# Two layer norms in a block-pipelined transformer tower: mean dropped, variance by ScalarE square with accumulator instead of VectorE statistics

## What is computed

```python
def _layernorm(x, axis=-1, eps=1e-5):
    m = jnp.mean(x, axis=axis, keepdims=True)
    v = jnp.var(x, axis=axis, keepdims=True)
    return (x - m) / jnp.sqrt(v + eps)

h = _L0_tok_ref(x, sqrt_eig, pct, 64)       # spectrum x Legendre table, then an inverse real FFT: [64, 256, 512]
h = h + _L0_attn_ref(_layernorm(h), K, temperature, bias)   # tanh logits, band of 12, softmax
h = h + _L0_ffn_ref(_layernorm(h), W, b)    # adds two one-hots in columns 128 to 159 of the marked rows
```

## Time and profile before

| | |
|---|---|
| three runs | 1578.57, 1577.88, 1573.31 us |
| the profiled execution | 1565.4 us; its span, first to last instruction, 1563.6 us |
| busy, share of the span | PE 89%, DVE 69%, ACT 43%, POOL 39% |
| stage 2's loop | about 497 to 1249 us of the span |
| mean granted clock of TensorE | 0.954 of full speed |

### The profile page before, as it was taken

How to read it: one execution, slowest core, us unless ns; L and a number is a source line. 1 busy time by engine, 2 the same in 40 slices (tenths; PEclk the granted TensorE clock), 3 DMA queues, 4 the chain that set the end, 5 groups by cost and what they waited for, 6 DMA issues and landing times. The chain is left out here.

```text
span 1563.6 us, 31624 instructions
## 1 busy us (share of the span) xinstructions
PE 1388.2 (89%) x9389; PEld 1217.4 (78%) x9389; DVE 1084.1 (69%) x2564; ACT 676.4 (43%) x1373; POOL 614.5 (39%) x1598
## 2 busy tenths in 40 slices
PE   4777777767999999999999999999999996599993
PEld 3666666657999999999999999999999995355541
DVE  1322222217899999999999999999999984466662
ACT  1222222213455455455455455455454452366672
POOL 2000000001466556655555665565565565121221
PEclk9799989988999999999999999999999998699997
DMA  9999999972122122212211211211221111000000
GB/s 374 428 428 428 428 428 429 428 265 71 56 78 73 70 69 74 77 68 69 80 68 68 81 68 68 81 68 68 74 75 68 43 42 42 23 9 8 8 3 3
DMA packets 58746, 210.57 MB, mean 135 GB/s; under 512 B 9412, under 2 KB 12176, under 8 KB 46288
## 3 DMA queue, kind: packets, MB, share of 16 engines
q1 hardware_dynamic: 47360, 172.29, 28.2%
q10 hardware_dynamic: 5200, 33.62, 5.4%
q0 software_dynamic: 6144, 4.14, 0.9%
HBM read 138.73 MB, written 73.07 MB: 135 GB/s over the span
## 5 line engine op out<-in xcount | busy, mean ns | idle before, releaser
L187 PE MATMUL s1b<-pg,cg 128*128 128x256 f32 x1024 | 246.9, 403 | 90.0 <-DVE cg L138 85.7
L187 PEld LDWEIGHTS s1b<-pg,cg 128*128 128x128 f32 x1024 | 204.9, 203 | 131.5 <-ACT stage L215 46.6
L426 PE MATMUL ps_kx<-xThi,Khi 128*128 128x256 f32 x1024 | 283.7, 277 | 4.0 <-DVE xTlo L678 4.0
L427 PE MATMUL ps_kx<-xTlo,Khi 128*128 128x256 f32 x1024 | 283.4, 277 | 0.0
L428 PE MATMUL ps_kx<-xThi,Klo 128*128 128x256 f32 x1024 | 283.4, 277 | 0.0
L138 DVE TENSOR_TENSOR cg<-xg,se 128x2048 f32<-128x2048 f32 x32 | 73.3, 2292 | 233.3 <-DMA pg<-in_pct_dram 211.0
L585 ACT ACTIVATE o<-h,sh,sc 128x512 f32<-128x512 f32 x128 | 97.5, 809 | 266.7 <-POOL sh L818 266.7
L426 PEld LDWEIGHTS ps_kx<-xThi,Khi 128*128 128x128 f32 x1024 | 193.2, 189 | 4.6 <-DVE xTlo L678 4.6
L428 PEld LDWEIGHTS ps_kx<-xThi,Klo 128*128 128x128 f32 x1024 | 192.9, 188 | 0.0
L427 PEld LDWEIGHTS ps_kx<-xTlo,Khi 128*128 128x128 f32 x1024 | 192.9, 188 | 0.0
L215 ACT COPY stage<-s1b 128x512 f32<-128x512 f32 x128 | 65.7, 598 | 234.0 <-PE s1b L187 234.0
(11 more groups left out here) (138 smaller groups left out, 3216.9 us busy)
## 6 DMA issues: line engine op xcount, KB each, us to landing
pg<-in_pct_dram SPq DMA_DIRECT2D x32, 2048.0 KB, 27.7
xg<-in_xs_dram SPq DMA_DIRECT2D x32, 1024.0 KB, 22.9
spec<-stage ACTq DMA_DIRECT2D x64, 512.0 KB, 8.5
xt<-spec SPq DMA_DIRECT2D x64, 512.0 KB, 3.6
out_dram<-o SPq DMA_DIRECT2D x64, 512.0 KB, 2.8
recs<-rec POOLq DMA_DIRECT2D x16, 160.0 KB, 16.1
recs<-rec,idx POOLq DMA_INDIRECT x128, 2.3
Kf<-in_K_dram SPq DMA_DIRECT2D x1, 1024.0 KB, 23.6
```

The source lines that it names most:

```text
L187: last = nc.tensor.matmul(bank[(b % 2) * 4 + m // 2][:, m % 2, :], cg[:, b % 2, m * 2 + h, :], pg[:, b, m * 2 + h, :], start=(h == 0), sto ...
L426: nc.tensor.matmul(out_ap, whi, mhi, start=(j == 0), stop=False)
L427: nc.tensor.matmul(out_ap, whi, mlo, start=False, stop=False)
```

## The change

Both norms take the mean as zero. The variance is the mean of the squares, made by two ScalarE activations for each sample and norm (Square of the row scaled by 1/sqrt(512), its sum accumulated into one column). For h2 these stand in ACT's slot after pThi and before xnhi; for h they stand at the end of ACT's slot, after o and before the next slot's tanh. All bn_stats and bn_aggr leave DVE, `off` leaves POOL, and xn and x2 are one multiplication without the subtraction.

```diff
+        squares = sb("squares", [P, 2, TILES, NLON])
+        var1 = sb("var1", [P, 4, TILES])
+        var2 = sb("var2", [P, 2, TILES])
+        zeros = sb("zeros", [P, TILES])
...
@@ ScalarE, slot: after pThi, before xnhi
+                if has(i - 2):
+                    n = i - 2
+                    act.wait_ge(dve_h2, n * 2 + 2)
+                    wait(act, pool_sc2, (n - 1) * 2)
+                    wait(act, act_var2, n * 2)
+                    for t in range(TILES):
+                        nc.scalar.activation(squares[:, 1, t], h2[:, k % 2, t], ACT.Square, scale=1.0 / math.sqrt(NLON),
+                                             accum_out=var2[:, k % 2, t:t + 1]).then_inc(act_var2, 1)
...
-                    act.wait_ge(pool_sc2, n * 3 + 3)
+                    act.wait_ge(pool_sc2, n * 2 + 2)
...
@@ ScalarE, slot: after o, last
+                if has(i + 2):
+                    n = i + 2
+                    act.wait_ge(dve_h, n * 3 + 3)
+                    wait(act, pool_rstd1, n - 3)
+                    wait(act, act_var1, n * 2)
+                    for t in range(TILES):
+                        nc.scalar.activation(squares[:, 0, t], h[:, (k + 2) % 4, t], ACT.Square, scale=1.0 / math.sqrt(NLON),
+                                             accum_out=var1[:, (k + 2) % 4, t:t + 1]).then_inc(act_var1, 1)
...
@@ VectorE, slot
-                        nc.vector.tensor_scalar(xn[:, r2, t], h[:, r4, t], mv1[:, r4, t, 0:1],
-                                                rstd1[:, r4, t:t + 1], ALU.subtract,
+                        nc.vector.tensor_scalar(xn[:, r2, t], h[:, r4, t], rstd1[:, r4, t:t + 1], None,
                                                 ALU.mult).then_inc(dve_xn, 1)
...
-                        nc.vector.bn_stats(bn2[:, t, :], h2[:, r2, t]).then_inc(dve_bn2, 1)
...
-                        nc.vector.bn_aggr(mv2[:, r2, t, :], bn2[:, t, :]).then_inc(dve_mv2, 1)
...
-                        nc.vector.bn_stats(bn1[:, t, :], h[:, r4, t]).then_inc(dve_bn1, 1)
...
-                        nc.vector.bn_aggr(mv1[:, r4, t, :], bn1[:, t, :]).then_inc(dve_mv1, 1)
...
-                        nc.vector.tensor_scalar(x2[:, r2, t, :], h2[:, r2, t, 0:P], mv2[:, r2, t, 0:1],
-                                                rstd2[:, r2, t:t + 1], ALU.subtract,
+                        nc.vector.tensor_scalar(x2[:, r2, t, :], h2[:, r2, t, 0:P], rstd2[:, r2, t:t + 1], None,
                                                 ALU.mult).then_inc(dve_x2, 1)
...
+            nc.vector.memset(zeros[:, :], 0.0).then_inc(consts_set, 1)
...
@@ GpSimd, slot
-                    pool.wait_ge(dve_mv1, n * 2 + 2)
+                    pool.wait_ge(act_var1, n * 2 + 2)
...
-                    pool.wait_ge(dve_mv2, n * 2 + 2)
+                    pool.wait_ge(act_var2, n * 2 + 2)
...
-                    nc.gpsimd.tensor_tensor(off[:, :], mv2[:, r2, :, 0], rstd2[:, r2, :], ALU.mult).then_inc(pool_sc2, 1)
-                    pool.wait_ge(pool_sc2, n * 3 + 2)
-                    nc.gpsimd.tensor_tensor(sh2[:, r2, :], dcT[:, :, bass.ds(n, 1)].rearrange("p t o -> p (t o)"), off[:, :],
+                    nc.gpsimd.tensor_tensor(sh2[:, r2, :], dcT[:, :, bass.ds(n, 1)].rearrange("p t o -> p (t o)"), zeros[:, :],
                                             ALU.subtract).then_inc(pool_sc2, 1)
```

More of the change, by code:

```diff
@@ L1 @@
 from contextlib import ExitStack
+import math
 import numpy as np
@@ L296, in stage2_blocks @@
         sh2 = sb("sh2", [P, 2, TILES])
-        off = sb("off", [P, TILES])
         mx = sb("mx", [P, TILES])
@@ L328, in stage2_blocks @@
         pe_rank = sem("pe_rank")
+        act_var1 = sem("act_var1")
+        act_var2 = sem("act_var2")
         act_od = sem("act_od")
@@ L341, in stage2_blocks @@
         dve_h = sem("dve_h")
-        dve_bn1 = sem("dve_bn1")
-        dve_mv1 = sem("dve_mv1")
         dve_xn = sem("dve_xn")
@@ L351, in stage2_blocks @@
         dve_h2 = sem("dve_h2")
-        dve_bn2 = sem("dve_bn2")
-        dve_mv2 = sem("dve_mv2")
         dve_x2 = sem("dve_x2")
@@ L742, in slot @@
                     n, r4 = i + 1, (k + 1) % 4
-                    pool.wait_ge(dve_mv1, n * 2 + 2)
+                    pool.wait_ge(act_var1, n * 2 + 2)
                     settled(pool)
-                    nc.gpsimd.tensor_scalar(ve[:, 0, :], mv1[:, r4, :, 1], EPS, None, ALU.add).then_inc(pool_ve, 1)
+                    nc.gpsimd.tensor_scalar(ve[:, 0, :], var1[:, r4, :], EPS, None, ALU.add).then_inc(pool_ve, 1)
                     pool.wait_ge(pool_ve, (max(n - 3, 0) if isinstance(n, int) else n - 3) + n + 1)
@@ L805, in slot @@
                     n, r2 = i - 2, k % 2
-                    pool.wait_ge(dve_mv2, n * 2 + 2)
+                    pool.wait_ge(act_var2, n * 2 + 2)
                     settled(pool)
-                    nc.gpsimd.tensor_scalar(ve[:, 1, :], mv2[:, r2, :, 1], EPS, None, ALU.add).then_inc(pool_ve, 1)
+                    nc.gpsimd.tensor_scalar(ve[:, 1, :], var2[:, r2, :], EPS, None, ALU.add).then_inc(pool_ve, 1)
                     pool.wait_ge(pool_ve, n + 1 + (min(n + 4, NB) if isinstance(n, int) else n + 4))
@@ L815, in slot @@
                     nc.gpsimd.tensor_scalar(sc2[:, r2, :], rstd2[:, r2, :], 1.0, None, ALU.add).then_inc(pool_sc2, 1)
-                    nc.gpsimd.tensor_tensor(off[:, :], mv2[:, r2, :, 0], rstd2[:, r2, :], ALU.mult).then_inc(pool_sc2, 1)
-                    pool.wait_ge(pool_sc2, n * 3 + 2)
-                    nc.gpsimd.tensor_tensor(sh2[:, r2, :], dcT[:, :, bass.ds(n, 1)].rearrange("p t o -> p (t o)"), off[:, :],
+                    nc.gpsimd.tensor_tensor(sh2[:, r2, :], dcT[:, :, bass.ds(n, 1)].rearrange("p t o -> p (t o)"), zeros[:, :],
                                             ALU.subtract).then_inc(pool_sc2, 1)
-            pool.wait_ge(consts_set, 5)
+            pool.wait_ge(consts_set, 6)
             pool.wait_ge(dcT_set, 1)
```

## The result

The changed kernel took 1640.32 us (median of four runs, 1635.03 to 1643.13) against 1578.22 us (four runs of the kernel before, the three above and 1579.51): a ratio of 1.0399, 95% interval 1.0376 to 1.0422, so 62 us slower. Forecast were 1648 us, 70 us slower, in a range of 1620 to 1680. The profiled execution has a span of 1633.2 us.

What follows compares the result with a forecast made beforehand. Two bounds of about equal length were taken: PE's work, 14.67 us a slot, and the ACT-POOL ring, 14.64. Terms of 1.37 - 0.37 - 0.10 + 0.30 = 1.20 us a slot added 70 us to 1577.9: 1648 us, range 1620 to 1680.

Steps and rivals of the forecast that it cites:

- The ring: Stage 2's closed chain on ACT and POOL from one tanh to the next, 14.64 us; whatever lengthens it lengthens the slot.
- Squares of h: On ACT between o and the next tanh, in the ring: a pair adds 1.37 us, bounds 1.16 and 1.63.
- off: Subtraction leaving POOL between sc and sh, with the wait behind it, in the ring: -0.37 us a slot.
- lg: POOL's step after tanh, in the ring, no longer overlapped by DVE's xnlo: -0.10 us a slot.
- The build of h against POOL: POOL's second-norm ve (L808) meeting DVE's L665 and L667, in the ring: +0.30 us a slot.
- Full lock-out: Rival: L808 always held through both DVE instructions L665 and L667, 1.51 us a slot, 1667 us; chance 0.15.
- Squares of h2: On ACT after pThi: 1.37 us hidden in 3.96 us of idle time, xTlo 0.9 us ahead of PE's keys.
- DVE's 2.7 us less: bn_stats and bn_aggr leaving DVE, 2.7 us a slot, costed at nothing because the ring hardly waits for DVE.
- The sum: All terms in the ring together: 1.20 us a slot over 60 slots, less some 2 us.
- PE keeps the beat: Rival: a quicker POOL chain makes good the squares, PE's 14.67 us bounds again, 1573 us; chance 0.09.
- Table loads: Rival: ACT reloads its table around Square, 1.28 us a slot in the ring, 1725 us; chance 0.03.
- The clock: Rival: PE's waits lower its granted clock from 2.4 GHz, 18.3 us a slot at 0.80, 1790 us; chance 0.03.

Runs made afterwards that it cites:

- the light runs: Matmuls of Klo with the rounded rows left out of keys: kernel before without 16 a slot 1610.09 us, without 8 1580.34 us; changed kernel without 16 1662.86 us.

## Why the prediction was right, and where it was off

*The bound.* The ring was read rightly from the timelines: tanh follows the squares without idle time, moving the squares out of it takes the loss away, a second pair adds its length again, and PE's weight load for rank waits 1.19 us a slot where about 1.3 was forecast. What I wrote of PE was too high: "about 14.67 us when it waits for nothing". It is 14.57. I had subtracted only the wait for acc that the list named; in the trace the two halves of the first rank product start 0.13 us apart while PE waits there, and 0.03 in the kernel with the squares behind tanh: another 0.1 us, which I had taken for work. So the two bounds did not stand side by side: the ring alone held the kernel before, by 0.18 us a slot.

*Squares of h.* 1.37 us was forecast from the exps' pair and measured is 1.23 (0.61 a square): mis-sized by 0.14, inside its bounds of 1.16 and 1.63. A square of h takes 0.617 us, where exp's 0.502 and my 0.185 for the columns made 0.69.

*off* gave 0.37, as forecast; *lg* gave 0.08 of the 0.10: before, DVE's xnlo was still running for 0.29 us when it began (the slot of the earlier trace rows), and in the changed kernel xnlo is over by then. Before:

```profile
806.93 1.22 DVE L717 TENSOR_TENSOR xnlo<-xn,xnhi 128x1024 fp32r<-128x1024 f32 x1
```

*The build of h against POOL.* +0.30 was forecast as the middle between getting in between the two h instructions (0) and being held through both (+0.61), and +0.22 was measured. The way was a third one: ve does get in between, 0.08 us sooner than before, and rstd2, which I had not costed, is held by the second instruction for 0.30 us. That the size comes near is luck: it was a mean of two cases for ve, and what cost was rstd2. Full lock-out of the second ve (L808 before the change, L797 after), a rival with 0.15, is out: it ends 0.08 us behind the first of the two h instructions. The rule that I had quoted from the Trainium skill, "SBUF — State Buffer", section "Who interferes with whom", an exclusion for the length of one instruction, holds here: ve lies against the first and rstd2 against the second.

*Squares of h2* were hidden from PE's keys, as forecast: no wait of PE for xThi or xTlo appears. "0.9 us to spare" was a statement about those keys, though, and I had not followed the lateness to DVE's end of the slot; alone, this half costs 21 us. In the full change the late od is what brings the build of h onto rstd2, so the 0.30 us there is a price of these squares.

*DVE's 2.7 us less* were rightly costed at nothing: the kernel with the first norm alone changed does more on DVE and takes the same time. But they do keep the late od from making DVE late for lg, ve and nmx.

*The sum* was 1.20 us a slot and is 1.07. The four terms that were forecast measured 1.00 together; the 0.12 between keyhi and pos, which had no term, brings the total nearer, and that is luck too. *PE keeps the beat*: out, by 1.07 us. *Table loads*: out, the trace still has one load, and squares, tanh and o leave no gap that a second, of 1.283 us, would need. *The clock* stayed at 1.00, as forecast for this change; the light runs show that it was nearer than I had written, since it fell where PE's wait was 1.5 us a slot (72.3 us in 49 waits) instead of 0.99, and its price there, 32 us, comes in single slots and not as a mean. With the squares of h made twice it fell too, at 1.68 us a slot (75.8 us in 45 waits), and the slots with a fall were no longer than the others.

## What to carry to other kernels

Before putting work on an engine that is half empty, find the place in its order: follow one round from an instruction back to itself, across engines, and look whether that round is closed without idle time. Where such a round sets the pace, work inside it costs its full length each time, however idle the engine is; the same work a few instructions away, where the engine waits for the other in any case, was free here, and the kernel then took 0.9% less than the one before. Work that hides in a wait still makes what stands behind it late; follow that too, to the end of the slot. A busy share of 99.9% does not show that an engine is the bound; taking a little of its work away does, as long as its clock stays up.

## What the runs showed of the hardware that was not expected

Less work for TensorE can make a kernel slower: with 1.81 us less in each slot, and longer waits, its granted clock fell to 1.2 GHz about every second slot, and 1578 us became 1610. With 0.91 us less, and waits of 0.82 us, it did not fall. A fall does not always cost time: with the squares of h made twice 14 of 47 slots had one and were no longer than the others.

GpSimd's small operations are held by DVE in more places than the statistics of the kernel before let one see. In the changed kernel, POOL's last acc takes 0.50 us instead of 0.19 in some slots, where it meets DVE's xn:

```profile
840.40 0.50 POOL L755 TENSOR_TENSOR acc<-acc,mask 128x1 f32<-128x1 f32 x1
```

```profile
840.38 0.87 DVE L637 TENSOR_SCALAR xn<-h,rstd 128x512 f32<-128x512 f32 x2
```

In the slot shown first, acc begins ahead of xn and is not held:

```profile
856.49 0.19 POOL L755 TENSOR_TENSOR acc<-acc,mask 128x1 f32<-128x1 f32 x1
```

```profile
856.68 0.87 DVE L637 TENSOR_SCALAR xn<-h,rstd 128x512 f32<-128x512 f32 x2
```

Where acc is held, PE's rank and ACT's pos are late: in the 23 of the 47 slots in which acc takes 0.49 to 0.50 us, from keyhi to pos it is 1.19 us; in the other 24 it is 0.94 to 0.95. That is the 0.12 us between keyhi and pos in the account above, read from the rows and not tried by itself.
